# First layer's experts: three fp32r products of high and low parts in place of one fp32 product

## The reference, cut to what matters

```python
x = x + L0_ffn(layernorm(x))
# L0_ffn, for a token t with normalized row h (256 numbers):
#   p = softmax(h @ router_w + router_b)          8 probabilities
#   e = argmax(p)
#   out = p[e] * (h @ expert_w[e] + expert_b[e])  expert_w: 8 x 256 x 256
```

## Time and profile before

| what | us |
|---|---|
| median of 3 runs | 6096.39 (6095.18 to 6096.58) |
| the profiled execution, its own time | 6100.48 |
| its span, first to last instruction | 6098.6 |
| TensorE busy | 5427.2 (89% of the span) |
| VectorE busy | 3993.1 (65%) |
| ScalarE busy | 2848.8 (47%) |
| GpSimd busy | 1761.1 (29%) |

### The profile page before, as it was taken

The page is one execution under the profiler, slowest core; times in us unless marked ns, Lnnn a source line. Parts: engine busy times, 40 slices in busy tenths (PEclk is TensorE's granted clock), DMA queues, the critical chain, the costliest instruction groups (busy, mean ns, idle before and its releaser), DMA issues.

```text
span 6098.6 us, 76361 instructions
## 1 busy us (share of the span) xinstructions
PE 5427.2 (89%) x29994; PEld 2957.3 (48%) x29994; DVE 3993.1 (65%) x6951; ACT 2848.8 (47%) x4524; POOL 1761.1 (29%) x1903
## 2 busy tenths in 40 slices
PE   7987999999977879999998989997958879799978
PEld 4443454454444645555555653336834444333355
DVE  5666767767676579888886257763267744788632
ACT  4553444444115466656564236672135555366600
POOL 3211333333024036454464022203422122222021
PEclk9997999999989989998999889998979989899989
DMA  1000000000000000000000000004410000000033
GB/s 53 1 3 1 1 1 1 1 1 1 21 30 1 8 28 1 1 1 1 1 1 1 10 1 1 1 1 155 166 35 1 1 17 1 32 1 1 32 101 106
DMA packets 39364, 125.10 MB, mean 21 GB/s; under 512 B 5588, under 2 KB 20940, under 8 KB 32990
## 3 DMA queue, kind: packets, MB, share of 16 engines
q1 hardware_dynamic: 28206, 67.70, 3.2%
q0 software_dynamic: 10800, 52.52, 2.5%
HBM read 99.42 MB, written 24.90 MB: 20 GB/s over the span
## 4 chain that ended last, share of the span: by engine, by line


## 5 line engine op out<-in xcount | busy, mean ns | idle before, releaser
L74 PE MATMUL PS<-SC 128*128 128x128 f32 (+14 forms) x14896 | 2814.3, 428 | 163.7 <-ACT SC L80 56.1
L80 ACT ACTIVATE SC<-PS 128x1024 f32<-128x1024 f32 (+7 forms) x2555 | 1933.7, 782 | 1892.6 <-PE PS L74 1560.7
L74 PEld LDWEIGHTS PS<-SC 128*128 128x128 f32 (+6 forms) x14896 | 1214.4, 129 | 1502.6 <-issue 603.7
L95 DVE TENSOR_REDUCE SC<-PS 128x1 f32<-128x512 f32 (+5 forms) x2368 | 1516.6, 680 | 603.0 <-PE PS L74 590.2
L83 POOL TENSOR_TENSOR SC<-SC 128x1024 f32<-128x1024 f32 (+3 forms) x892 | 1190.0, 1344 | 1490.0 <-ACT SC L80 1245.7
L74 PE MATMUL PS<-AR 128*128 128x128 bf16 (+6 forms) x4000 | 1121.6, 393 | 64.2 <-DVE SC L83 16.2
L74 PEld LDWEIGHTS PS<-AR 128*128 128x128 f32 (+2 forms) x4000 | 599.5, 174 | 461.3 <-issue 269.5
L77 PE MATMUL PS<-AR,SC 128*104 128x128 bf16 (+3 forms) x4664 | 518.4, 254 | 322.4 <-DVE SC L86 156.3
L74 PE MATMUL PS<-SC,AR 128*128 128x512 f32 (+7 forms) x1938 | 760.4, 516 | 46.1 <-POOL SC L83 12.8
L77 PEld LDWEIGHTS PS<-AR,SC 128*104 128x104 bf16 (+3 forms) x4664 | 402.1, 135 | 537.6 <-DVE SC L86 142.3
L80 ACT ACTIVATE SC<-SC 128x512 f32<-128x512 f32 (+7 forms) x870 | 445.1, 563 | 454.0 <-DVE SC L86 217.0
(11 more groups left out here) (82 smaller groups left out, 2165.3 us busy)
## 6 DMA issues: line engine op xcount, KB each, us to landing
SC<-in_pk11e SPq DMA_DIRECT2D x8, 1152.0 KB, 5.9
SC<-in_pk11e SPq DMA_DIRECT2D x8, 1028.0 KB, 5.1
xg<-SC SPq DMA_DIRECT2D x16, 512.0 KB, 6.8
SC<-yg SPq DMA_DIRECT2D x16, 512.0 KB, 7.6
yg<-AR SPq DMA_DIRECT2D x8, 512.0 KB, 5.8
AR<-in_pk SPq DMA_DIRECT2D x2, 1562.0 KB, 8.0
AR<-in_pk SPq DMA_DIRECT2D x2, 1538.0 KB, 12.9
AR<-in_pk SPq DMA_DIRECT2D x6, 512.0 KB, 4.9
```

What stands on the lines that cost most here:

```text
L74: return Step(self.real and self.real.matmul(*a, **k))
L80: return Step(self.real and self.real.activation(*a, **k))
L95: return Step(self.real and self.real.tensor_reduce(*a, **k))
```

## The change

It makes 14 pieces of 128 x 512: eight of the expert weights (4096 columns) and six of the normalized x of tiles 4 to 15. ScalarE copies each into a high part (fp32r), and VectorE subtracts it from the whole for a low part (fp32r). ScalarE makes all high parts in a row, right after the router's Exp. VectorE makes one low part after the sums of each of groups 1 to 14. Tiles 0 to 3 are multiplied as before. For tiles 4 to 15 each chunk's fp32 product gives way to three fp32r products: x high by w high, x high by w low, x low by w high; TensorE waits at tiles 4, 8 and 12 for the low parts of that set. The parts take 14336 words of scratch, and the scratch of the next stage is moved by 16800 words.

```diff
--- before.py
+++ after.py
@@ -1320,6 +1320,9 @@
 
 
 
+
+
+
     next = None
 
     def __init__(self, K):
@@ -1329,6 +1332,12 @@
         self.ew = w[:, 0:4096].rearrange("p (c e n) -> p c e n", c=2, e=8)
         self.rw = w[:, 4096:4112].rearrange("p (c n) -> p c n", c=2)
         self.rb = w[0:1, 4112:4120]
+        self.wh, self.wl = [K.scr.take([2, 8, D], F32R) for _ in range(2)]
+        self.xh, self.xl = [K.scr.take([2, 3, 512], F32R) for _ in range(2)]
+
+        flat = lambda v, c, k: v[:, c].rearrange("p e n -> p (e n)")[:, 512 * k:512 * k + 512]
+        self.pieces = [tuple(flat(v, c, k) for v in (self.ew, self.wh, self.wl)) for c in range(2) for k in range(4)]
+        self.pieces += [(K.XNT[:, c, 512 * k + 512:512 * k + 1024], self.xh[:, c, k], self.xl[:, c, k]) for k in range(3) for c in range(2)]
         self.eb = K.scr.take([D], F32, 0, 8)
         self.eb_ready = K.load("d_eb")
         self.router = Router(K, "r2")
@@ -1407,9 +1416,18 @@
                     e.wait_ge(K.vv, ("2 sum", n - 6, 1))
                 elif n == 0:
                     e.wait_ge(K.av, "2 bb")
-                for c in range(2):
-                    t = e.matmul(PS[:, self.bank(n), :], K.XNT[:, c, 128 * i:128 * i + 128],
-                                 self.ew[:, c, 2 * e2:2 * e2 + 2, :].rearrange("p e n -> p (e n)"), start=c == 0, stop=c == 1)
+                pair = lambda v, c: v[:, c, 2 * e2:2 * e2 + 2, :].rearrange("p e n -> p (e n)")
+                if i < 4:
+                    for c in range(2):
+                        t = e.matmul(PS[:, self.bank(n), :], K.XNT[:, c, 128 * i:128 * i + 128], pair(self.ew, c), start=c == 0, stop=c == 1)
+                else:
+                    if e2 == 0 and i % 4 == 0:
+                        e.wait_ge(K.vv, ("2 low", 7 + 2 * (i // 4)))
+                    part = lambda v, c: v[:, c, i // 4 - 1, 128 * (i % 4):128 * (i % 4) + 128]
+                    for c in range(2):
+                        e.matmul(PS[:, self.bank(n), :], part(self.xh, c), pair(self.wh, c), start=c == 0, stop=False)
+                        e.matmul(PS[:, self.bank(n), :], part(self.xh, c), pair(self.wl, c), start=False, stop=False)
+                        t = e.matmul(PS[:, self.bank(n), :], part(self.xl, c), pair(self.wh, c), start=False, stop=c == 1)
                 t.then_inc(K.mm, ("2 experts", n))
             if i % 4 == 1:
                 self.pe_gates(e, i // 4)
@@ -1438,6 +1456,8 @@
 
         e.activation(self.one, K.ones[:, 0:1], ACT.Exp).then_inc(K.av, "2 table")
         self.router.act_softmax(e)
+        for m, (whole, high, _) in enumerate(self.pieces):
+            e.activation(high, whole, ACT.Copy).then_inc(K.av, ("2 high", m))
         for k in range(4):
             e.wait_ge(K.mm, ("2 GT", k))
             if k >= 2:
@@ -1483,6 +1503,10 @@
                         e.wait_ge(K.vv, ("2 sum", n, 0) if k else ("2 sum", n - 1, 1))
                     e.scalar_tensor_tensor(out=X[:, i, :], in0=PS[:, self.bank(n), 256 * k:256 * k + 256], scalar=G[:, i, 2 * e2 + k:2 * e2 + k + 1],
                                            in1=X[:, i, :], op0=ALU.mult, op1=ALU.add).then_inc(K.vv, ("2 sum", n, k))
+                if 1 <= n <= len(self.pieces):
+                    whole, high, low = self.pieces[n - 1]
+                    e.wait_ge(K.av, ("2 high", n - 1))
+                    e.tensor_tensor(low, whole, high.bitcast(F32), ALU.subtract).then_inc(K.vv, ("2 low", n - 1))
             if self.next is not None and i % 4 == 3:
                 self.next.tick_dve(e, i // 4)
         if self.next is not None:
@@ -1587,6 +1611,8 @@
 
 
 def stages_3(K):
+
+    K.scr.take([16800])
     st = BatchAttention(K)
     norm = follow(K, Norm(K, "n3", [layer(K.X, st.O)]))
     K.tail = Project(K, "o3", st.O, st.wo, K.X)
```

## The result

The changed kernel takes 6078.4 us (median of 7 runs, 6071.3 to 6086.2) against 6096.6 for the kernel before, measured beside it (7 runs, 6093.9 to 6102.4). The ratio is 0.9968 with an interval of [0.9957, 0.9978]: 19.5 us faster, between 13 and 26 (the two medians by themselves differ by 18.2). The forecast was 6081.2 us, 15.2 off.

The account below looks back on a forecast made before the run. The prediction took TensorE to bound the expert stage. Only the products counted, 48 x (1.72 - 1.4025) = 15.2 us, with both kinds of parts hidden at no cost: 6096.4 - 15.2 = 6081.2 us, range 6075 to 6087.

Parts of the forecast that it names:

- The bound: Expert stage: TensorE alone sets its length, so what products of tiles 4 to 15 save comes off the total.
- The products: Tiles 4 to 15: 48 groups go from 1.72 to 1.40 us at 0.234 a product, gaining 15.2 us.
- the prediction's own sign of being wrong: Expert stage: forecast is wrong if, among other signs, the products' distance is not 0.234 us.
- Rival 2: Tiles 4 to 15: products run at one pass' pace, 0.215 us; 20.6 us off, 6075.8; chance 0.08.
- The high parts: ScalarE after the router's Exp: 14 copies of 0.62 us, 8.7 us, hidden in a 12.89 us gap; cost nothing.
- The low parts: VectorE, first four tiles: 14 subtractions of 0.68 us, 9.5 us, cost zero with 1.2 us to spare.
- Rival 3: Tiles 0 to 7: VectorE becomes the bound, TensorE waits some 3 us; 6084; chance 0.08.
- Rival 4: fp32r products: 187 ns weight loads add to each product, 33 us slower, 6129; chance 0.03.
- Later sets: Sets of four tiles after the first shrink to 24.9 us; VectorE's work fits and TensorE still bounds.
- The rest: Outside the products: no transfer added or moved, moved scratch costs nothing, the chain after the last product keeps its lengths.
- Rival 5: Behind the stage: gain partly given back to clock changes, or products run at 256-column pace; about 6085; chance 0.05.
- The total: Whole kernel: 15.2 us off the 6096.4 us median gives 6081.2 us.

Follow-up runs that it names:

- e5: Changed kernel with tiles 4 to 7's x parts in QA and tiles 8 to 11's products reordered; stage 103.76 us, runs from 6066.9 to 6090.8 us.
- e3: Changed kernel with each low part computed twice, the second time into spare scratch; stage 105.65 us against 103.25.
- e4: Changed kernel without the third product, x low by w high, in tiles 4 to 15; 26.2 us off in all, stage 25.7 shorter.
- e2: Changed kernel with all parts made and scratch moved, but every product fp32; 6098.1 us beside 6098.2 for the kernel before, ratio 1.0003.
- e1: Changed kernel with tiles 4 to 7 back in fp32, so 32 groups instead of 48 in fp32r; 17.7 us faster than the kernel before.
- e6: Changed kernel extended to all 16 tiles in fp32r, VectorE making the weights' parts while waiting for the router's logits; 6061.3 us, ratio 0.9938.
- e8: Kernel before, all fp32 and old scratch, with 26 groups leaving out their second chunk; 20.7 us faster [13, 28].
- e9: Kernel before, all fp32 and old scratch, with 13 groups leaving out their second chunk; 12.2 us faster [7, 18].
- e7: The changed kernel repeated without a change; 9 runs from 6069.4 to 6087.9 us, median 6080.7, ratio 0.9969 against the kernel before.

## Why the prediction was right, point by point

**The bound.** Right: no idle time of TensorE in the stage, and the whole of the stage's gain reached the next stage, behind the same 2.03 us wait.

**The products.** The mechanism was right, the pace mis-sized: 0.234 us was taken from the second layer's block, 0.227 was measured. The sum by it is 48 x (1.72 - 6 x 0.227) = 17.2 us, of which 16.84 came; the rest lies in the first products after the switch from fp32, after the gates and after the biases, where the next record starts 0.63, 0.32 and 0.34 us later instead of 0.227. The step that failed is "I take 0.234, as it is the same shape": the block had the same shape, but its operands in two places, and e5, with the x parts moved to QA, got 0.233. By the prediction's own sign of being wrong, "if the products' distance is not 0.234", this term failed, by 3%.

**Rival 2, one pass' pace.** Half of its condition came true, its price did not. The 0.234 did belong to the other block's operands, but what takes its place is 0.227 and not 0.215, so the gain was 16.84 us and not 20.6. The Trainium skill's page "TensorE: Matmul & The Clock Gate", section "Back-to-back issue gap", gives about 216 ns by its formula for a single warm product and about 131 ns for a sustained stream of them, and neither depends on where the operands lie. The traces here disagree with both for fp32r, with 0.227 and 0.233.

**The high parts.** Right: hidden in ScalarE's gap, 7.38 us in place of 8.7 (0.52 us from one start to the next; the 0.62 taken from the earlier trace rows was the length of one instruction, and neighbours overlap).

**The low parts.** The zero was right, the way to it too cautious. A low part does not add its 0.68 us to 1.08: a pair of sums followed by it holds VectorE for 0.91 us and the low part for 0.60, 1.51 together. Two sums one behind the other take 0.54 each. That the second of a pair, or the next pair, is held up by the one before it unless other work stands between fits these numbers; it was not tried by itself. The first norm's step was shorter too (1.93 us from 1618.97 to 1620.90, not 3.44). So VectorE finished the sums of group 16 some 3 us ahead of the reckoning: counted from the stage's entry, the forecast had 1622.4 - 1585.2 = 37.2, and it was 1621.9 - 1587.7 = 34.2. With the 1.2 us to spare that makes about 4 us of slack, and e3 measures it: 3.8 us. Rival 3 fell with it, as the changed kernel's TensorE has no idle time; e3 is what it would have looked like.

**Rival 4, exposed weight loads.** Fell: six products with six loads take 1.37 us.

**Later sets.** 24.39 us against 24.9, by the same pace. VectorE's pairs fit, and e4 shows how far: at 21.95 us a set it is the bound.

**The rest.** "Moved scratch costs nothing" is right as far as e2 can show (between 4 us faster and 7 slower). "After the last product the chain has the same instructions and lengths" is right in its instructions and wrong in its lengths: the stages behind ran 6.8 us shorter in one execution of the changed kernel and 4.4 longer in another. Rival 5 had the mechanism, later stages meeting the clock's changes otherwise, but as a fixed loss. What the runs show is a spread, of both signs.

**The total.** The median's 6078.4 lies 2.8 below the forecast; 1.6 of it are the stage's (16.84 for 15.2), and the remaining 1.2 are within the spread. The spread itself was the weakest number of the prediction: three runs of before lay within 1.4 us, seven runs of the changed kernel within 15. The range of 12 us, 6075 to 6087, held the median, not each run: two of the seven lie below it. That the median came within 3 us is in part luck, as the rest alone differs by 11 us between the two profiled executions of this one kernel.

**What stays open.** The totals of e1 and above all e6 fall by more than their stages: by 6.5 and 15.4 us, where the intervals reach some 6.5 and 8. The moved scratch alone does not do it (e2), nor does a shorter stage alone (e8, e9, the latter with e1's stage to 0.1 us), and e4, with fp32r as well, has no surplus (26.2 against 25.7). What carries the rest of a profiled execution can be read, from the windows between the first turn and the end (before, e6, e8; columns as in the earlier trace rows):

```profile
1705.31:6098.60 4393.29, 3839.58 (x20237) 2171.58 (x20235) 2840.31 (x5190) 2138.29 (x3542) 1305.01 (x1520) 0.92 0.07 26
```

```profile
1688.81:6071.10 4382.29, 3827.98 (x20237) 2164.12 (x20235) 2838.53 (x5190) 2137.80 (x3542) 1304.70 (x1520) 0.93 0.08 26
```

```profile
1680.70:6079.80 4399.10, 3845.92 (x20237) 2172.98 (x20235) 2839.12 (x5191) 2138.28 (x3542) 1303.11 (x1520) 0.92 0.07 26
```

Against before, e6 is 11.0 us shorter there and e8, counted from the first turn, 5.8 longer, and TensorE is busy 11.6 us less and 6.3 more for the same 20237 products, while VectorE's time differs by under 2 us. e6, the shortest, has the higher granted clock, 0.93. The mean granted clock of e6's five executions is 0.937 to 0.939, that of the 18 of before beside them 0.934 to 0.938. So in these profiles the surplus goes with the clock of the later stages; in e7's two profiles TensorE has a smaller part of it, 7.9 of 11.2 us. What in the stage steers that clock, if anything does, was not found, and the cause of the surplus stays open.

## What to carry to other kernels

Replacing each fp32 product by three fp32r ones on high and low parts pays 0.35 us for a group of two products of 128 x 128 by 512 where TensorE bounds, if the parts are made in idle time of other engines just ahead of it; look for such time before the stage too, as e6 did with VectorE's 12 us. Take a product's pace from a row of the same shape with its operands in the same places. And judge a change of 0.3% by its stage's length in the trace, which repeated to 0.01 us here, before the total, which varies by 15 us between seven runs of the changed kernel and by 24 between the nine of e5.

## What was not expected of the hardware

- An fp32r product of 512 columns with its own weight load takes 0.227 us with both operands in QB and 0.233 with the stationary one in QA.
- 14 copies of 128 x 512 on ScalarE come 0.52 us apart though each is 0.61 long; on VectorE a low part between two pairs of sums makes the pair cheaper, 0.91 in place of 1.08 us.
- The same program ran 2750 products in 408.0 us at a granted clock of 0.97 and in 413.0 at 0.95. The first 110 us, the same program in each, were granted 0.86 in the changed kernel's profile and 0.97 in those of before and e1. Whole executions follow the clock too: e5's shortest took 6066.9 us at a mean of 0.939, its longest 6090.8 at 0.934.
